# A Mamba block and an expert block on one core: the first batch's front alone, and the weight products inside the first batch's scans

## The reference, cut to what matters

```python
# block 1, a selective state space model (d = 256, di = 512, N = 16 states, rank 16)
h = x * rsqrt(mean(x*x) + EPS) * norm_scale
xs, res = split(h @ w_in);  res = silu(res);  xs = silu(causal_conv(xs, conv_w, conv_b))
delta, B, C = split(xs @ w_xproj);  delta = softplus(delta @ w_dt + b_dt)
deltaA = exp(delta[..., None] * -exp(A_log));  deltaBx = (delta * xs)[..., None] * B[:, :, None, :]
ys = linear scan over the 512 rows of  state = deltaA * state + deltaBx
y = einsum('blcn,bln->blc', ys, C);  out = x + ((y + xs * D) * res) @ w_out
# block 2, two branches (forward and inverse) of 8 experts of rank 64
Q = x @ W_Q.T;  K = x @ W_K.T;  invQ = Q @ W_inv.T;  invK = K @ W_inv.T
prod = (Q @ V) * cumsum(K @ W)          # per expert, in both branches
weights = softmax(gelu(Q @ router_w1.T + b1) @ router_w2.T + b2)
out = einsum(prod * weights, U) + weights @ b, over the row's number;  (fwd + alpha * inv) @ W_O.T
```

## Time and profile before

| | |
|---|---|
| median of 3 runs | 2573.84 us (2567.31 to 2573.85) |
| the profiled execution, its own time | 2574.76 us |
| its span in the trace | 2572.9 us |
| busy, share of the span | PE 85%, DVE 89%, ACT 66%, POOL 68% |
| first scan starts, last scan starts | 95.8 us, 2451.8 us |

### The profile page before, as it was taken

How to read it: one execution, slowest core, us unless ns; L and a number is a source line. 1 busy time by engine, 2 the same in 40 slices (tenths; PEclk the granted TensorE clock), 3 DMA queues, 4 the chain that set the end, 5 groups by cost and what they waited for, 6 DMA issues and landing times.

```text
span 2572.9 us, 35477 instructions
## 1 busy us (share of the span) xinstructions
PE 2179.5 (85%) x9268; PEld 1305.7 (51%) x9268; DVE 2291.9 (89%) x3172; ACT 1704.3 (66%) x3353; POOL 1752.1 (68%) x1227
## 2 busy tenths in 40 slices
PE   5666788888898988888898888989888888888788
PEld 2434455454554645455464545546454555546454
DVE  1599999999999999999899999999999999999941
ACT  3555585958668594876758586685948767595643
POOL 0759586767858676695867768586766958677611
PEclk9776899999999999999899999999999999999999
DMA  5011010101002011110101011020101001011100
GB/s 123 28 46 30 20 58 25 58 26 54 31 20 64 25 56 29 54 30 26 59 25 55 29 54 31 19 64 25 57 28 54 30 26 58 25 50 32 35 1 17
DMA packets 83383, 101.58 MB, mean 39 GB/s; under 512 B 23480, under 2 KB 49872, under 8 KB 83168
## 3 DMA queue, kind: packets, MB, share of 16 engines
q1 hardware_dynamic: 83168, 99.06, 13.1%
HBM read 90.13 MB, written 8.91 MB: 38 GB/s over the span
## 4 chain that ended last, share of the span: by engine, by line
DVE 33%; issue 28%; POOL 15%; PE 15%; ACT 4%; DVEq 1%; POOLq 0%; ACTq 0%
DVE h L1259 15%; POOL bx L714 9%; DVE yT L1275 9%; PE bank L744 8%; PE stateT L913 3%; DVE xs L1163 3%; DVE prod L1234 2%; PE bank L888 2%; POOL x_back L646 1%; POOL scratch L630 1%; POOL scratch L636 1%; DVE xs L1175 1%; ACT decay L1119 1%; DVE rows L1187 1%; ACT cum_sb L1084 1%
## 5 line engine op out<-in xcount | busy, mean ns | idle before, releaser
L714 POOL TENSOR_TENSOR bx<-dx,B_rows 128x1024 f32<-128x1024 f32 x512 | 1206.6, 2363 | 379.3 <-DVE h L1259 374.7
L1259 DVE TENSOR_TENSOR_SCAN h<-decay,bx 128x512 f32<-128x512 f32 x1024 | 1237.7, 1209 | 57.4 <-ACT decay L1119 50.9
L1119 ACT ACTIVATE decay<-delta,decay_rate 128x512 f32<-128x512 f32 x1024 | 706.6, 692 | 487.3 <-DVE h L1259 477.3
L913 PE MATMUL stateT<-ident,h 128*128 128x128 f32 x4096 | 668.8, 295 | 264.9 <-DVE h L1259 179.5
L913 PEld LDWEIGHTS stateT<-ident,h 128*128 128x128 f32 x4096 | 498.8, 149 | 614.5 <-issue 333.2
L1275 DVE SCALAR_TENSOR_TENSOR yT<-stateT,C_tok,yT 128x512 f32<-128x512 f32 x960 | 697.8, 727 | 34.3 <-PE stateT L913 29.7
L744 PE MATMUL bank<-hT,w_in_sb 128*128 128x512 f32 x512 | 247.5, 621 | 34.7 <-DVE xs L1163 33.7
L744 PE MATMUL bank<-k_to_expert,cumT 128*128 128x512 f32 x512 | 266.4, 647 | 4.1 <-DVE prod L1234 4.1
L744 PE MATMUL bank<-q_to_expert,xnT 128*128 128x512 f32 x512 | 248.0, 608 | 1.9 <-ACT C_tok L1007 1.9
L1084 ACT ACTIVATE cum_sb<-bank,gate 128x64 f32<-128x64 f32 x1024 | 222.7, 328 | 35.6 <-PE bank L744 33.3
L888 PE MATMUL bank<-expert_to_out,prodT 128*128 128x256 f32 x1024 | 241.8, 379 | 0.0
(11 more groups left out here) (162 smaller groups left out, 2412.9 us busy)
## 6 DMA issues: line engine op xcount, KB each, us to landing
B_rows<-B_scratch SPq DMA_DIRECT2D x256, 256.0 KB, 3.2
x_front<-in_L_attn_x SPq DMA_DIRECT2D x16, 512.0 KB, 4.6
x_back<-in_L_attn_x SPq DMA_DIRECT2D x16, 512.0 KB, 4.1
out<-x_back SPq DMA_DIRECT2D x16, 512.0 KB, 3.3
w_in_sb<-in_L_attn_w_in SPq DMA_DIRECT2D x1, 1024.0 KB, 5.9
h<-in_L_ffn_V_fwd SPq DMA_DIRECT2D x2, 256.0 KB
h<-in_L_ffn_W_inv_exp SPq DMA_DIRECT2D x2, 256.0 KB
h<-in_L_ffn_W_fwd SPq DMA_DIRECT2D x2, 256.0 KB
```

What stands on the lines that cost most here:

```text
L714: pool.tensor_tensor(bx[use % BX_RING][:, :, :], dx[q.parity][:, 2 * half:2 * half + 2, :], row, ALU.mult).then_inc(s_bx.step(f"{n},{half} ...
L913: last = pe.transpose(stateT[j % 2][:, c * P:(c + 1) * P], h[n % 2][:, c, j * P:(j + 1) * P], ident[:, :])
L1119: act.activation(decay[c % 2][:, :], delta[q.parity][:, c, :], ACT.Exp, scale=decay_rate[:, c, n:n + 1]).then_inc(s_exp.step(f"{n},{c}"), 1)
L1259: dve.tensor_tensor_scan(h[n % 2][:, c, :], decay[c % 2][:, :], bx[(2 * n + c // 2) % BX_RING][:, c % 2, :], 0.0, ALU.mult, ALU.add).then_ ...
```

## The change

x and the weights of the front are loaded first, on a semaphore of their own (front_ld), and only PE's first `xs` and ACT's first `hT` wait for it. PE waits for no weights at its start. ACT's `exp` of A_log (`rates`) and DVE's constants move from the prologue to beat 24 of period q = -1, ahead of the `hT` copies in ACT's queue. The 22 jobs move into period q = 0. They take one of the four banks, where it is free, and their staged weights lie in tiles that batch 0 needs only after its scans. ACT's copy of a job stands 6 beats after its products. By the rule in the diff and the new beats the jobs come to PE at beats 1, 4, 7, 10, 13, 16, 19, 22, 49, 53, 56, 59, 62, 65, 70, 73, 78, 81, 86, 89, 97 and 104, none of them while the front of batch 1 holds the banks. The waits for the jobs go from the head of the scans to SP's load of x_back (moved for batch 0 from slot 12 to slot 15), PE's first `rt` and DVE's first `r`, all later. POOL's bx for groups 0 and 1 waits for `dx1` only, and for groups 2 and 3 for `dx3`; `dx3` now stands behind the first bx. The bank of `res3` in period q = -1 is now that of `xs1`. And many tasks get new beats.

```diff
-JOBS_FROM, JOBS_EVERY = 60, 3
+JOBS_FROM, JOBS_EVERY = 1, 3
+KEPT_AFTER = 6
+READ_WITHIN = 14
+LATE = 24
...
-    ("F", "ag", "dve"): (8,),
+    ("F", "ag", "dve"): (9,),
-    ("F", "hT", "pe"): (17, 26),
-    ("F", "hT", "act"): (24, 31),
-    ("F", "x", "sp"): (79,),
+    ("F", "hT", "pe"): (20, 28),
+    ("F", "hT", "act"): (28, 30),
+    ("F", "x", "sp"): (93,),
-    ("F", "res", "pe"): (36, 38, 41, 66),
-    ("F", "res", "act"): (38, 45, 47, 70),
-    ("F", "silu", "act"): (71,),
+    ("F", "res", "pe"): (36, 38, 41, 64),
+    ("F", "res", "act"): (36, 43, 44, 68),
+    ("F", "silu", "act"): (70,),
-    ("F", "dt", "pe"): (82, 89, 100, 107),
-    ("F", "dt", "act"): (89, 90, 107, 114),
-    ("F", "ex", "act"): (91, 95, 107, 119),
-    ("F", "ln", "act"): (92, 96, 109, 119),
-    ("F", "w", "pool"): (101, 105, 117, 126),
-    ("F", "w2", "pool"): (101, 109, 121, 126),
-    ("F", "d1", "dve"): (94, 104, 119, 122),
+    ("F", "dt", "pe"): (85, 89, 101, 107),
+    ("F", "dt", "act"): (89, 95, 106, 113),
+    ("F", "ex", "act"): (91, 95, 107, 118),
+    ("F", "ln", "act"): (92, 96, 108, 119),
+    ("F", "w", "pool"): (101, 105, 117, 124),
+    ("F", "w2", "pool"): (101, 107, 121, 126),
+    ("F", "d1", "dve"): (95, 104, 119, 122),
-    ("B", "logit", "pe"): (341,),
-    ("B", "logit", "act"): (344,),
+    ("B", "logit", "pe"): (339,),
+    ("B", "logit", "act"): (343,),
-    ("B", "mx", "dve"): (346,),
-    ("B", "sub", "pool"): (354,),
+    ("B", "mx", "dve"): (345,),
+    ("B", "sub", "pool"): (353,),
-    ("L", "ag", "dve"): (460,),
+    ("L", "ag", "dve"): (457,),
-    ("F", "dx", "pool"): (103, 111, 126, 127),
+    ("F", "dx", "pool"): (103, 114, 126, 128),
...
                 for at in range(BEATS):
                     scan_part(q, at // 8, at % 8)
+                    beat = at if name == "pe" else at - KEPT_AFTER
+                    if job_part and q.turn is None and q.const == 0 and beat in job_beats:
+                        i = job_beats.index(beat)
+                        place = job_banks[i]
+                        before = held[place]
+                        job_part(i, Use(bank[place], before[0].sem, before[0].done(before[1], before[2])) if before else Use(bank[place], w_pool, 2))
+                        if name == "pe":
+                            held[place] = (JobSteps, q, i)
...
-        stage_V = [h[0][:, 0:2, :], h[0][:, 2:4, :]]
-        stage_W = [h[1][:, 0:2, :], h[1][:, 2:4, :]]
-        stage_U = [bx[0][:, :, :], bx[1][:, :, :]]
+        stage_V = [cum_sb, prod]
+        stage_W = [[xnT[:, 0, :], xnT[:, 1, :]], [prodT[:, 4 * t:4 * t + 4, :].rearrange("p a b -> p (a b)") for t in range(DT)]]
+        stage_U = [[cumT[:, 0, :], cumT[:, 1, :]], [x_back[0][:, 2 * t:2 * t + 2, :].rearrange("p a b -> p (a b)") for t in range(DT)]]
...
-        job_bank = decay + stateT
-        job_beats = [JOBS_FROM + JOBS_EVERY * i for i in range(len(jobs))]
+        fills = [(beat, bank_of(stage, task, k, Batch(1))) for beat, tasks in enumerate(plan("pe"))
+                 for periods, stage, task, k in tasks if periods == 0]
+        def bank_is_free(at, place):
+            return (not any(place == b and at - READ_WITHIN <= beat < at + KEPT_AFTER + 2 for beat, b in fills)
+                    and not any(place == b and at < beat + KEPT_AFTER + 2 for beat, b in zip(job_beats, job_banks)))
...
             def load_x_back(batch):
+                if batch.turn is None and batch.const < 2:
+                    sp.wait_ge(w_act, len(jobs))
...
-                if q.turn is None and q.const == 0 and n == 0 and half == 0:
-                    pool.wait_ge(w_act, len(jobs))
-                if n == 0 and half == 0:
-                    pool.wait_ge(f_pool.sem, f_pool.done(q, "dx3"))
+                if n == 0:
+                    pool.wait_ge(f_pool.sem, f_pool.done(q, f"dx{2 * half + 1}"))
...
             def prologue():
-                pe.wait_ge(w_ld, 16 * N_WEIGHTS[0])
                 pe.wait_ge(w_pool, 2)
...
             def xs_task(b, c, use):
+                if b.turn is None and b.const == 0 and c == 0:
+                    pe.wait_ge(front_ld, 16 * N_FRONT[0])
...
             def hT_task(b, t, use):
                 act.wait_ge(f_pe.sem, f_pe.done(b, f"hT{t}"))
+                if t == 0 and b.turn is None and b.const == 0:
+                    act.wait_ge(front_ld, 16 * N_FRONT[0])
...
             def scan_part(q, n, beat):
-                if q.turn is None and q.const == -1 and 8 * n + beat in job_beats:
-                    keep_combined(job_beats.index(8 * n + beat))
+                if q.turn is None and q.const == -1 and 8 * n + beat == LATE:
+                    rates()
```

More of the change, by code:

```diff
@@ L468, in program @@
         job([(0, D, bT[:, t, :], woT[:, t, :], t == 0, t == DT - 1) for t in range(DT)], bias_to_out[:, :], D, j_bT, None, 2 * KE)
-        job_bank = decay + stateT
-        job_beats = [JOBS_FROM + JOBS_EVERY * i for i in range(len(jobs))]
-        assert job_beats[-1] < BEATS
+        fills = [(beat, bank_of(stage, task, k, Batch(1))) for beat, tasks in enumerate(plan("pe"))
[3 more added lines that the diff above has]
+                    and not any(place == b and at < beat + KEPT_AFTER + 2 for beat, b in zip(job_beats, job_banks)))
+        job_beats, job_banks = [], []
+        for at in range(JOBS_FROM, BEATS - KEPT_AFTER):
+            if len(job_beats) < len(jobs) and (not job_beats or at >= job_beats[-1] + JOBS_EVERY):
+                free = [place for place in range(4) if bank_is_free(at, place)]
+                if free:
+                    last = lambda place: max([beat for beat, b in zip(job_beats, job_banks) if b == place], default=-1)
+                    job_beats.append(at)
+                    job_banks.append(min(free, key=last))
+        assert len(job_beats) == len(jobs), len(job_beats)
         block = ctx.enter_context(nc.Block())
-        N_WEIGHTS, N_EXPERT = [0], [0]
+        N_FRONT, N_WEIGHTS, N_EXPERT = [0], [0], [0]
         @block.sync
@@ L565, in scan_part @@
                         row_of_B(q, slot + BB_RING - 1)
-                    if slot == 12:
+                    if slot == (NS - 1 if q.turn is None and q.const == 0 else 12):
                         load_x_back(q)
@@ L736, in combine_weights @@
                         k = src.shape[0]
-                        last = pe.transpose(job_bank[i % 4][:, mm[0]:mm[1]], src, ident[0:k, 0:k])
+                        last = pe.transpose(use.bank[:, mm[0]:mm[1]], src, ident[0:k, 0:k])
                     else:
-                        last = pe.matmul(job_bank[i % 4][0:parts, mm[0]:mm[1]], mm[2], mm[3], start=mm[4], stop=mm[5])
+                        last = pe.matmul(use.bank[0:parts, mm[0]:mm[1]], mm[2], mm[3], start=mm[4], stop=mm[5])
                 last.then_inc(w_pe, 1)
@@ L818, in rt_task @@
                 br, m = k // 2, k % 2
+                if k == 0 and b.turn is None and b.const == 0:
+                    pe.wait_ge(w_act, len(jobs))
                 if k == 0:
@@ L893, in scan_part @@
             def scan_part(q, slot, beat):
-                if q.turn is None and q.const == -1 and 8 * slot + beat in job_beats:
-                    combine_weights(job_beats.index(8 * slot + beat))
                 if beat % 2:
@@ L1129, in prologue, with constants @@
             def prologue():
+                pass
+            def constants():
                 dve.wait_ge(w_rate, 1)
@@ L1180, in r_task @@
                 if j == 0:
+                    if b.turn is None and b.const == 0:
+                        dve.wait_ge(w_act, len(jobs))
                     dve.wait_ge(xb_in[b.parity], b.half_count(16, 16))
@@ L1244, in scan_part @@
                 k = beat // 2
+                if q.turn is None and q.const == -1 and 8 * slot + beat == LATE:
+                    constants()
                 if beat % 2 == 0:
```

150 lines of the change are left out of this document (81 added, 69 removed), and 8 rows, old and new, of the table TIMETABLE.

## The result

The kernel after takes **2588.99 us** (median of 5 runs, 2586.18 to 2589.59), the kernel before in the same session 2573.85 (2567.31 to 2582.53). The ratio is 1.0053, 95% interval [1.003, 1.0076]: slower by 15 us, where 2539 was forecast and 2557 was the end of the range. The profiled execution took 2589.49 us, its span is 2587.6.

What follows compares the result with a forecast made beforehand. DVE was taken as the bound, busy 144 of 150 us in a steady period. From 2574.8 us, the start took off 27.4, the jobs added 2.0 and the new beats took off 10: 2539, range 2517 to 2557.

Steps and rivals of the forecast that it cites:

- steps (a) to (f): The start, from loading x to the first scans: six stretches of the chain, together giving 27.4 us.
- the rival of a later last load: At the start: the last small load lands after 15.77, shrinking a 10.6 us gain; folded into the range, no chance given.
- Step (b): In the start, from the first xs product to silu's table load: 16.8 us instead of 19.3.
- Step (c): In the start, from silu to the projection's copy: 8.7 us instead of 9.4, with 1.7 added for idle PE.
- step (f): In the start, from POOL's first w to the first bx: 15.7 us instead of 23.4; first scan at 67.2.
- The jobs in period 0, +2.0: The moved jobs of products on PE and copies on ACT cost 2.0 us, by DVE waiting for PE's transposes.
- the lower bound of the text: For the jobs in period 0: they cost nothing, or less, since a busier PE has a higher clock.
- the rival that PE does not keep up: In period 0, jobs at clock 0.50 put 13 us or more on DVE: 2552 to 2568; chance 0.11.
- The new beats, -10: In 15 fronts and 16 backs: d1's wait of 0.97 goes, 14.5 us in all, of which 10 was taken.
- The first, that the beats give nothing: The start gives its 27 us, but new waits replace the old one in the beats: 2549; chance 0.24.
- The slower one: PE's logit at beat 83 waits for gelu and delays transposes; ends slower than before, 2591 at 3 a period; chance 0.04.
- a steady pair longer than before: Named as refuting the forecast beyond the start; the forecast had a pair of steady periods shorter by about 1.3.

Runs made afterwards that it cites:

- the plan halves: The kernel after with old beats for entries whose old beat lies at 80 to 127: 2567.92 us; with old beats for those before 80 instead: 2586.45 us.
- both forms tried: The d1 add as tensor_tensor, and as scalar_tensor_tensor: the latter gave 2588.35 us in the kernel after, 2621.4 in the kernel before with dx1 at 114.

## Why the prediction was wrong, by its steps

**The start, steps (a) to (f): right, 2.1 us too much.** The first product stood at 17.38 (17.5 forecast), the table load at 35.42 (34.3), the first softplus at 46.75 (45.1), the first `w` at 50.59 (49.0), the first scan at 69.44 (67.2). The start gave 25.3 for 27.4. The exp of A_log came at 15.87, so the rival of a later last load did not come true. Step (b) was 1.2 short: after 2.68 us of idle PE, the first sixteen products took 10.07 us instead of 9.22. Step (c): the projection after 3.91 us of idle time took 6.17. I had taken 5.3 from the earlier trace rows; by the rule of the Trainium skill (TensorE: Matmul & The Clock Gate, Part 1: The HAM clock gate) it would have been 7.2. The measurement lies midway. In step (f) the last two `d1` were held by POOL, at 1.73 us each, the first sight of what came later.

**The jobs in period 0, +2.0: right.** With the new beats period 0 was 138.3 us with the jobs and 136.0 without, so they cost 2.3. DVE waited 6.6 us for PE, more than the 4 foreseen and under the 8 that would have refuted it. The clock of that period rose to 0.83 (0.64 in both kernels without jobs in it), as the lower bound of the text had it, and PE's busy time rose from 91.6 to 104.1 and not by the 33 us of the sum. DVE's wait for decay fell from 6.9 to 2.3. So the rival that PE does not keep up did not come true with this plan; with the old beats the same jobs cost 6.2 (145.3 against 139.0).

**The new beats, -10: the step that failed.** The text followed one wait, `d1` of group 0 for `w2`, and it went nearly as said: over the fourteen periods `d1` waits 1.1 us for POOL instead of 13.2, and 5.1 for ACT that it had not waited before, so 7.0 are won. The waits for decay fall as well, from 42.2 to 30.1, where the text expected more of them. What the sum lacked was any term for an instruction of DVE that itself takes longer. The step was made by waits alone, and bounded by waits: "a loss of about 1 a period" was the worst it allowed. The measured loss is 39.3 in fourteen periods, 2.8 a period, of which the held add is 2.05. The rest is a second price that the text put at nothing, PE's: 28 us more of waiting for transposes, of which 12 go when the add and the late product are both mended. In time, the runs put the two beats at 46 us. No wait in the trace of before shows that price. What showed it was the 1.10 us that POOL stood idle for `d1`, which the new plan fills with bx, and the durations of `d1` in the same trace: a median of 0.69, and a maximum of 1.73 us where POOL was in the middle of a `dx`. The diff had the line, `dx1` from 111 to 114, and the text did not ask what POOL would be doing instead while DVE adds. With the two beats mended (`dx1` back at 111 and the third `cum` product back at 104), the fourteen periods are 2084.9, which is 3.8 better than before: the sign of the step was right for the rest of the plan, its size less than half of the 10.

**The rivals.** The first, that the beats give nothing because new waits replace the old one, had the right doubt and not the size. The slower one came true in its sign and not in its place. It put the price at PE's logit at beat 83; the plan halves show the loss in the late stretch, where that beat is too, yet with that beat left as it is the two edits give it all back. Its own sentence, "have to add more than 2.2 net in each of 14 periods", was the right measure: 2.8 were added. "Nothing in the rows gives so much" was true of the rows shown and wrong of the trace: no row gave the spread of `d1`'s durations, and the text did not ask for one. What the text named as a refutation, "a steady pair longer than before", is what happened.

**The sum, mended.** For the kernel with both beats mended the parts of the table give 25.2 (start) + 1.0 (period 0) + 3.8 (fourteen periods) - 1.2 (tail) = 28.8. That is only the difference of the two spans, 2572.9 and 2544.2, by its parts; beside the forecast's 27.4 - 2.0 + 10 it shows the start and the jobs about right and the beats 6 too much. The forecast of 2539 lies 4 us under this kernel's median.

## What to carry to other kernels

A plan that fills one engine's idle time can take it from another: look for every DVE instruction with two operands in SBUF, and ask what GpSimd does in that moment, before and after. Compare the longest and the median duration of a group, not only its waits; where the longest is far above the median, look for what holds it. And when one mended cause gives back less than its own duration, look at what now waits right behind it before calling the cause wrong: here the two edits gave 7.5 and 3.5 us by themselves and 46 together.

## What was not expected of the hardware

A DVE instruction that reads two operands from SBUF stands still while a tensor_tensor of GpSimd runs: 2.71 us instead of 0.66, in both forms tried. In every one of the 17 long adds of the kernel after it ends 0.55 us after GpSimd's instruction, less than the 0.66 that it takes alone. It holds the other way round as well: at 66.56 in the start of the kernel after, the bx began while the held `d1` had yet to run, and took 2.78 us instead of 2.36. Scans and sums with one operand in PSUM ran beside the same bx at their usual 1.21 and 0.73 us.

Standing still for 1.8 us costs more than 1.8 us: the one held add in each of 15 fronts cost the kernel before 3.1 us a front. Part of it is PE's clock. In the front shown PE waited 1.01 and 0.68 us for the DVE that had stood still, and then ran four products in 3.14 us at a granted clock of 0.60, instead of 1.88 at 1.00. With the add moved by two beats, the time at the lower clock is back at 169 us from 266. That the gaps are what lowered the clock is argued from this order of events.
